# TensorE reads a whole round's expert numbers into registers with one load, in place of four at every fourth tile

## The reference

```
g = xt @ Wg[e];  u = xt @ Wu[e];  h = silu(g) * u;  y = h @ Wd[e]      # 128 -> 344 -> 128
out = sum over the two chosen experts of weight * y
```

## Time and profile before

| | us |
|---|---|
| median of 3 runs | 848.82 |
| lowest, highest | 848.80, 850.25 |
| the profiled execution, its own time | 843.71 |
| its span, first to last instruction | 841.0 |
| PE busy | 649.6 (77%) |
| DVE busy | 739.6 (88%) |
| ACT busy | 506.9 (60%) |
| POOL busy | 580.0 (69%) |

### The profile page before, as it was taken

The page is one execution under the profiler, slowest core; times in us unless marked ns, Lnnn a source line. Parts: engine busy times, 40 slices in busy tenths (PEclk is TensorE's granted clock), DMA queues, the critical chain, the costliest instruction groups (busy, mean ns, idle before and its releaser), DMA issues.

```text
span 841.0 us, 12622 instructions
## 1 busy us (share of the span) xinstructions
PE 649.6 (77%) x3545; PEld 465.1 (55%) x3545; DVE 739.6 (88%) x1147; ACT 506.9 (60%) x1091; POOL 580.0 (69%) x487
## 2 busy tenths in 40 slices
PE   4438688878778877787967877986876889898992
PEld 2124455545355536764657635863554556788992
DVE  1376998989999999999999999999999898686676
ACT  2545895876678577565856567464864775444441
POOL 1095675677977797688958897689855995456542
PEclk9659898989989898997889989897877899999996
DMA  6933233222323335543364336532423520123139
GB/s 177 269 97 101 91 111 111 83 88 90 115 75 101 104 105 182 160 134 114 114 192 135 107 101 189 154 124 97 132 86 104 179 85 24 45 55 93 54 102 272
DMA packets 80295, 99.92 MB, mean 119 GB/s; under 512 B 10263, under 2 KB 48099, under 8 KB 80211
## 3 DMA queue, kind: packets, MB, share of 16 engines
q1 hardware_dynamic: 75907, 90.21, 35.9%
q0 software_dynamic: 4320, 8.92, 3.0%
HBM read 87.56 MB, written 15.35 MB: 122 GB/s over the span
## 4 chain that ended last, share of the span: by engine, by line
DVE 36%; PE 33%; issue 18%; ACT 6%; POOL 4%; DMA 2%; SPq 1%; DVEq 1%; ACTq 0%; POOLq 0%
DVE state L1092 18%; PE work_front L1270 4%; DVE product L1102 4%; PE y L1310 4%; PE up L1432 2%; PE up L1421 2%; PE work_front L1276 2%; PE y L1306 2%; PE gate L1414 2%; POOL inflow L833 2%; DVE stats L1022 2%; ACT decay L956 1%; DVE silu_m L1235 1%; DVE arena L1067 1%; PE work_side L1354 1%
## 5 line engine op out<-in xcount | busy, mean ns | idle before, releaser
L833 POOL TENSOR_TENSOR inflow<-du,b_wide 128x1024 f32<-128x1024 f32 x128 | 315.5, 2468 | 145.1 <-DVE product L1102 92.1
L1092 DVE TENSOR_TENSOR_SCAN state<-decay,carry,inflow 128x512 f32<-128x512 f32 x192 | 234.8, 1264 | 6.5 <-ACT decay L956 6.5
L1102 DVE TENSOR_TENSOR product<-state,c_wide 128x1024 f32<-128x1024 f32 (+1 forms) x93 | 138.9, 1494 | 4.4 <-PE y L1306 3.3
L956 ACT ACTIVATE decay<-arena,a_neg 128x512 f32<-128x512 f32 x128 | 86.6, 688 | 60.6 <-DVE state L1092 56.8
L1306 PE MATMUL y<-ident,product 128*128 128x128 f32 x664 | 106.5, 305 | 20.5 <-DVE product L1102 20.5
L1306 PEld LDWEIGHTS y<-ident,product 128*128 128x128 f32 x664 | 87.4, 158 | 62.5 <-issue 34.7
L956 ACT ACTIVATE decay<-delta_odd,a_neg 128x512 f32<-128x512 f32 x128 | 86.5, 688 | 56.2 <-DVE state L1092 56.0
L863 POOL DMA_INDIRECT y_dram<-y_rows,x_rows x71 | 81.6, 1149 | 55.9 <-ACT y_rows L1012 49.2
L1310 PE MATMUL y<-h_rows,ident 128*128 128x512 f32 x180 | 100.9, 652 | 7.1 <-ACT h_rows L921 6.5
L857 POOL DMA_INDIRECT row_dram<-m_tok,place x64 | 74.2, 1159 | 24.4 <-issue 12.9
L1092 DVE TENSOR_TENSOR_SCAN state<-decay,inflow 128x512 f32<-128x512 f32 x64 | 74.5, 1203 | 6.1 <-ACT decay L956 3.6
(11 more groups left out here) (232 smaller groups left out, 1342.5 us busy)
## 6 DMA issues: line engine op xcount, KB each, us to landing
b_wide<-bc_dram SPq DMA_DIRECT2D x128, 256.0 KB, 3.3
c_wide<-bc_dram SPq DMA_DIRECT2D x93, 256.0 KB, 3.5
w_stage<-gate_up_dram SPq DMA_DIRECT2D x26, 344.0 KB, 4.4
x_rows<-row_dram SPq DMA_DIRECT2D x71, 65.0 KB, 2.1
arena<-gate_up_dram SPq DMA_DIRECT2D x8, 344.0 KB, 4.2
x_tok<-in_x SPq DMA_DIRECT2D x8, 256.0 KB, 5.8
out<-x_tok SPq DMA_DIRECT2D x7, 256.0 KB, 4.9
inflow<-y_dram SPq DMA_DIRECT2D x6, 256.0 KB, 4.5
```

Source lines behind the costliest of these rows:

```text
L833: e.tensor_tensor(inflow[:, key % 3], du[:, c % 2], b_wide[:, key % ROW_SLOTS:key % ROW_SLOTS + 1, :].to_broadcast([P, HALVES, CHUNK]), AL ...
L956: e.activation(decay_bank[h][:], delta[c % 2][:, h, :], ACT.Exp, scale=a_neg[:, h, n:n + 1]).then_inc(S["decay"], 1)
L1092: e.tensor_tensor_scan(state[:, key % STATE_SLOTS, h, :], decay_bank[h][:], inflow[:, key % 3, h, :], 0.0 if c % (SEQ // CHUNK) == 0 else ...
L1102: e.tensor_tensor(product[:, key % 2, :, :wide], state[:, key % STATE_SLOTS, :, :wide], c_wide[:, key % ROW_SLOTS:key % ROW_SLOTS + 1, :wi ...
```

## The change

`picks` takes a number of entries `n`, which is `PICKS` (4) unless it is given. PE's `down` gives `MOST_TILES` (22), so it loads at tile 0 of each round, and takes all the entries that the round has: 9, 8, 8, 8, 8, 8 and 22. It keeps them in registers through the round. SP's and DVE's loads stay as they were, as do all waits, matmuls and transfers. PE's loads are 7 in place of 19; the entries read are 71 as before.

```
-        def picks(engine, table, k, j, most):
+        def picks(engine, table, k, j, most, n=PICKS):
 
-            return nc.values_load_multi_w_load_instructions(table[0:1, k, j:min(j + PICKS, TILES[k])], engines=(engine,), min_val=0, max_val=most,
+            return nc.values_load_multi_w_load_instructions(table[0:1, k, j:min(j + n, TILES[k])], engines=(engine,), min_val=0, max_val=most,
...
-                    if j % PICKS == 0:
-                        experts = picks(mybir.EngineType.PE, expert_i, k, j, EXPERTS - 1)
+                    if j % MOST_TILES == 0:
+                        experts = picks(mybir.EngineType.PE, expert_i, k, j, EXPERTS - 1, MOST_TILES)
                     e.wait_ge(S["moe_h"], key + 1)
...
-                                     w_down[:n, bass.ds(experts[j % PICKS], 1), q, :].rearrange("p o d -> p (o d)"), start=q == 0, stop=q == NF - 1)
+                                     w_down[:n, bass.ds(experts[j % MOST_TILES], 1), q, :].rearrange("p o d -> p (o d)"), start=q == 0, stop=q == NF - 1)
```

## The result

The kernel is slower by about 8 us: the median is 856.65 us (5 runs, 854.44 to 861.48) against 848.82 (5 runs, 847.88 to 850.25), a ratio of 1.0098 with the interval 1.0076 to 1.0119. The forecast was 856.3. The profiled execution took 861.48 us (span 859.7).

The account below looks back on a forecast made before the run. DVE was taken to bound the scans and PE's matmul stream the tail. Terms 4.16 - 1.35 + 1.67 + 0.93 + 2.05 gave +7.5 us on 848.82, so 856.3 us, range 849.0 to 861.

Parts of the forecast that it names:

- part 1: Round 7, ahead of the first `down`: one 22-entry load of 5.16 us replaces one of 1.00, +4.16 us.
- part 2: Round 7, loads removed: -0.45 us each at tiles 4, 8 and 12, -1.35 together; nothing at tiles 16 and 20.
- part 4: Round 5, first `down`: eight entries off the 16-byte boundary instead of four, counting in full, +0.93 us.
- part 5: Rounds 1 and 3, in the scans: longer loads delay DVE's `logits`, +1.14 and +0.91 us; lower end 0.
- part 6: Rounds 2, 4 and 6: two wide reads for one, at most +0.23 us each, hidden by waits and matmuls, 0.
- the single price: Loads starting 8 bytes off a 16-byte multiple: 308 ns, then 231 for each further entry; 5.16 us for 22.
- Rival A: Loads go over to wide reads once the address is a multiple of 16: sum +0.3, 849.1 us; chance 0.18.
- Rival B: A load costs by instruction, not entry; 22 entries take about 1.00 us: 847.5 to 845.2 us; chance 0.06.
- Part 3: Round 7, behind the long load's idle: one stretch of 3.40 us at the lower clock, 1.2 GHz, +1.67 us.
- Rival C: Long load as forecast, but the clock stays up and the scans absorb their delay: +3.7, 852.6 us; chance 0.14.

Follow-up runs that it names:

- E8: The changed kernel run again unchanged, beside the kernel before: 858.71 us, ratio 1.0093, profiled 858.38.
- E7: The kernel before run again unchanged, as a measure of scatter: 850.99 us, ratio 1.0010, profiled 849.85.
- E9: The kernel before with table rows of 24 entries, so loads of four start on multiples of 16 bytes, run a second time: 850.17 us, ratio 0.9992.
- E2: The changed kernel with table rows of 24 entries, so long loads start on multiples of 16 bytes: 852.04 us, ratio 1.0033 to the kernel before.
- E3: The kernel before with PE's long load in round 7 only, loads of four in rounds 1 to 6: 855.78 us, ratio 1.0079.
- E4: The kernel before with PE's long loads in rounds 1 to 6 only, loads of four in round 7: 855.25 us, ratio 1.0065.
- E5: The kernel before with PE loading one entry at every tile, 71 loads: 851.26 us against 850.47, ratio 1.0020.
- E10: The changed kernel with table rows of 24 entries, a second run of E2: 851.68 us, ratio 1.0023 to the kernel before.

## Why the prediction was right

The time difference, taken apart by when the same instruction of DVE comes in both traces. The first column of numbers is the forecast, the next E8 minus E7, the last the first profiles of the two kernels.

```
                                   forecast   E8 - E7   first pair
part 1 + 3: long load and clock      +5.83     +5.93      +5.94
part 2: loads gone, tiles 4, 8, 12   -1.35     -1.40      -1.35
part 4: round 5                      +0.93     +1.00      +0.98
part 5: round 1                      +1.14     +2.2       +1.13
part 5: round 3                      +0.91     +0.83      +0.62
part 6: rounds 2, 4, 6                0         0          0
sum of these                         +7.5      +8.6       +7.3
the rest (not of the loads)                     0.0      +10.4
```

The rest in E8 - E7 is +0.77 before the first load, +0.79 in round 6, +0.1 between rounds 1 and 3, and -1.7 behind tile 12, in the waits for the fetches at the merges and the end. That it comes to 0.0 is chance. The +0.79 needn't be the load of eight: E9, with loads of four, has +0.75 in the same stretch. In the first pair the rest is mostly the 5.2 us of round 6 (E7) and some 3.5 between 560 and 700 us.

The forecast of 856.3 met the median of 856.65, and that is in part luck. The parts are found in the traces, each in its place, but the intervals are 3 to 5 us wide, the time over E7 is 7.7 us by the medians and 8.5 by the two profiles, and round 1 costs 1.1 or 2.2 us from one execution to the next.

*Part 1* held in its price and its place: 5.31 us for 5.16, idle of 4.49 for 4.35. The step that decided it was taking the single price for all 22 entries. *Rival A* is refuted by the same row: a change to wide reads in the middle would have given 1.7 us. E2 shows that a load of 22 comes near that (1.85 us) only if it starts on the boundary. *Rival B* is refuted by the nine, eleven and 22 entries, which took 2.38, 2.73 and 5.31 us.

The Trainium skill, "Runtime: NRT & Kernel Launch", section "Instruction fetch mechanics", has some 200 ns per register, also in bulk. The traces come near it where the start lies 8 bytes off (5307 ns for 22 entries, 241 for each), and don't agree on a multiple of 16: eight entries in 612 ns and 22 in 1852.

*Part 2* held: the period went from 2.57 to 2.12 us. For tiles 16 and 20 I forecast nothing, as the merges wait for fetches; behind tile 12 E8 gains another 0.7 us up to the merges, but E7's waits for the fetches there differ from the first profile's by more (1.62 us at one of them, 0.45 in the earlier trace rows), so this step is neither confirmed nor refuted. In the first pair 0.44 us gained at tile 16 are gone at the next merges, as forecast.

*Part 3* held at +1.63 and 1.6, and 2.5 in E3. *Rival C* is refuted in both its halves: the clock fell behind or in every idle of 4.5 us (all three traces; in E3 before the idle was over), and the scans gave back nothing of rounds 1 and 3.

*Part 4* held, *part 6* too (the loads of eight took 0.26 to 0.28 us more, for 0.23, and no wait shows it). *Part 5* is the term that was off: behind round 1's longer load the clock can stay down for 8 us more, which costs as much again as the load. It did so in E4 and E8 and not in the first profile; what decides it is open, as the low stretch of E9 shows. I had the row that warned of it, slow matmuls behind the idle of 1.07 us, used it only for rival C, and added no clock term for round 1.

The parts made separately don't add up by their times: E3 has 6.7 us and E4 5.5, the whole 8.3. By the traces they are 5.5 and 3.9, together 9.4, against the 8.6 of E8 - E7, and the longer low stretch of E3 (2.5 us in place of 1.6) is what they differ by. The timed intervals are 3 to 5 us wide, and that is how much room a sum of times has.

## What to carry to other kernels

Before loads of registers from a table are made longer, look at their durations by start address: here four entries cost 333 or 1002 ns, and the difference is the row length of the table, 22 or 24 entries. Next ask how much of a load the queued work of its engine covers, since loads within that cover leave no idle, however many they are (in E5's tail one of 0.3 us at every tile left none on PE), while one beyond it stops the engine and may bring the clock down with it. And where a change is worth under 1%, run the kernel before once more with a profile, before a stretch of the first one is believed: the same code stood 5 us apart in one stretch.

## What the runs showed of the hardware

- A load into PE's registers took 300 to 308 ns for one entry (the median of E5, and the one of the kernel before). Started 8 bytes off a multiple of 16 it took 1002 (4 entries, the median), 1937 to 1987 (8), 2361 to 2377 (9), 2733 and 2735 (11) and 5298 to 5317 ns (22). Started on it: 332 (4, the median), 587 to 617 (8), 1057 (9), 1852 and 1856 (22). A load that started off it didn't go over to wide reads on the way. The bytes are counted from the start of the table, whose own address no trace shows; other offsets than 0 and 8 were not run.
- In a stream that kept PE full, idles of 1.92 us (twice) and 4.5 us (three times) were followed by 0.50 of the clock for 3.2 us or more; one of 1.03 us (E2, E10) was not. Behind the shorter idle the fall came about 1 us after the work had begun again.
- One program's executions stood 4.9 us apart in one stretch (22.87 and 27.77 us), in which, in the longer, ACT waited for something that the trace doesn't name.
